# A decoder layer with attention, a selective scan and a quantised feed-forward block: which queues move the rotated heads, and when the feed-forward weights are loaded

## What is computed

```python
x = x + attention(layernorm(x))          # 32 heads of 64, 8 k/v heads, rope on q and k, causal
x = x + ssm(ctx_1024, layernorm(x))      # 16 states: conv, projections, scan over time, gate silu(z)
x = x + ffn(layernorm(x))                # 704 hidden, integer weights of gate, up and down

def step(state, xs):                     # of the ssm, for each of 256 channels and 16 states
    d_t, B_t, C_t, u_t = xs
    dA = jnp.exp(d_t[..., None] * A)
    state = state * dA + (d_t * u_t)[..., None] * B_t[:, None, :]
    y_t = jnp.einsum('ben,bn->be', state, C_t)
    return (state, y_t)

def _qlinear(x, wq, scale):
    W = (wq.astype(jnp.float32) - ZERO_POINT) * scale[:, None]
    return jnp.einsum('bsd,hd->bsh', x, W)
gate = jax.nn.silu(_qlinear(x, wq_gate, s_gate))
up = _qlinear(x, wq_up, s_up)
return _qlinear(gate * up, wq_down, s_down)
```

## Time and profile before

| | before |
|---|---|
| the profiled execution's own time | 523.78 us |
| its span | 522.0 us |
| PE busy | 414.5 us (79%) |
| DVE busy | 366.6 us (70%) |
| ACT busy | 271.0 us (52%) |
| POOL busy | 221.3 us (42%), the issue of DMAs not counted |
| mean granted clock of PE | 0.912 |

### The profile page before, as it was taken

One profiled execution on the slowest core, in us unless ns is written; L12 is line 12 of the kernel. 1 busy time (PEld: TensorE's weight loads), 2 busy tenths in 40 slices (PEclk: granted clock), 3 DMA queues, 4 the chain that ended last, 5 costly groups with the idle time before them and its releaser, 6 DMA issues.

```text
span 522.0 us, 7681 instructions
## 1 busy us (share of the span) xinstructions
PE 414.5 (79%) x2604; PEld 325.4 (62%) x2636; DVE 366.6 (70%) x485; ACT 271.0 (52%) x779; POOL 221.3 (42%) x234
## 2 busy tenths in 40 slices
PE   3648987188768697987889799978998894659996
PEld 1433666166656476866777688757887773447774
DVE  2774357257999885897798679858767999755442
ACT  0514587046556465755666658645556665433321
POOL 1741232206464666446446635635464474310000
PEclk9787789687889799998999989989999997779999
DMA  9325324703151415201430521323042130000000
GB/s 223 74 56 96 113 51 131 230 10 98 37 170 55 156 31 153 96 11 46 133 102 24 144 91 48 76 87 102 21 133 74 57 102 0 2 0 21 20 22 20
DMA packets 51110, 40.63 MB, mean 78 GB/s; under 512 B 32280, under 2 KB 43744, under 8 KB 51072
## 3 DMA queue, kind: packets, MB, share of 16 engines
q1 hardware_dynamic: 40864, 34.48, 23.2%
q0 software_dynamic: 4096, 4.20, 3.4%
q10 hardware_dynamic: 6112, 1.47, 1.4%
HBM read 26.36 MB, written 1.18 MB: 53 GB/s over the span
## 4 chain that ended last, share of the span: by engine, by line
PE 33%; DVE 17%; issue 15%; SPq 12%; POOL 9%; DMA 7%; ACT 5%; ACTq 2%; DVEq 0%; POOLq 0%
PE ps_s L1041 6%; SPq L303 6%; PE ps_p L1028 6%; PE ps_p L1243 5%; DMA qt<-rc 4%; POOL rc L418 4%; DVE state L793 4%; PE ps_s L1228 3%; DVE nmax L711 3%; PE ps_p L1141 3%; PE ps_r L1095 3%; DVE state L786 3%; DMA kt<-rc 3%; SPq L266 2%; POOL y L424 2%
## 5 line engine op out<-in xcount | busy, mean ns | idle before, releaser
L493 ACT ACTIVATE prob<-ps_s,nmax 128x256 f32<-128x256 f32 (+1 forms) x256 | 104.8, 444 | 72.6 <-DVE nmax L711 72.6
L424 POOL TENSOR_TENSOR y<-y,state 128x1024 f32<-128x1024 f32 x32 | 80.3, 2510 | 112.2 <-DVE state L799 112.2
L418 POOL TENSOR_TENSOR rc<-rc,rs 128x512 f32<-128x512 f32 x40 | 57.7, 1442 | 104.0 <-DVE rs L699 70.4
L711 DVE TENSOR_REDUCE nmax<-ps_s 128x2 f32<-128x512 f32 (+1 forms) x96 | 60.3, 682 | 45.1 <-PE ps_s L1052 45.1
L499 ACT ACTIVATE pt<-ps_r 128x512 f32<-128x512 f32 x96 | 53.6, 593 | 58.1 <-PE ps_r L1095 54.5
L793 DVE TENSOR_TENSOR_SCAN state<-decay,state 128x1024 f32<-128x1024 f32 x32 | 81.5, 2546 | 2.3 <-ACT decay L519 1.2
L1041 PE MATMUL ps_s<-kt,qt 64*128 64x256 f32 (+1 forms) x512 | 55.5, 360 | 30.7 <-DMA qt<-rc 30.7
L1028 PE MATMUL ps_p<-xt_all,wq 128*128 128x256 f32 x256 | 71.2, 427 | 9.1 <-DVE rs L703 6.4
L1041 PEld LDWEIGHTS ps_s<-kt,qt 64*128 64x128 f32 x512 | 47.1, 201 | 38.2 <-DMA qt<-rc 32.5
L266 POOL DMA_DIRECT2D qt<-rc x128 | 63.8, 504 | 9.7 <-POOL rc L418 9.5
L1141 PE MATMUL ps_p<-wo,attn_t 128*128 128x256 f32 x256 | 61.7, 389 | 7.7 <-DVE x L816 4.1
(11 more groups left out here) (110 smaller groups left out, 531.1 us busy)
## 6 DMA issues: line engine op xcount, KB each, us to landing
bc<-bc_scratch SPq DMA_DIRECT2D x32, 512.0 KB, 4.7
qt<-rc POOLq DMA_DIRECT2D x128, 32.0 KB, 1.7
qt<-rc SPq DMA_DIRECT2D x128, 32.0 KB, 2.0
kt<-rc SPq DMA_DIRECT2D x64, 32.0 KB, 1.8
kt<-kt SPq DMA_DIRECT2D x8, 256.0 KB, 3.0
wo<-wo_t SPq DMA_DIRECT2D x1, 2048.0 KB, 10.9
wq<-wqkv_t SPq DMA_DIRECT2D x24, 64.0 KB, 2.6
xs<-x SPq DMA_DIRECT2D x1, 1024.0 KB, 8.1
```

The source lines that it names most:

```text
L418: nc.gpsimd.tensor_tensor(rc[:, r % 2, :, :], rc[:, r % 2, :, :], rs[:], ALU.add).then_inc(rope_add, 1)
L424: nc.gpsimd.tensor_tensor(y[:, v % 2, :], y[:, v % 2, :], state[:, v % 2, :], ALU.add).then_inc(state_free, 1)
L493: nc.scalar.activation(o, i, ACT.Exp, bias=nmax[:, r, c:c + 1], accum_out=rsum[:, r, GRP + head:GRP + head + 1]).then_inc(exp_done, 1)
L711: nc.vector.tensor_reduce(nmax[:, u % 2, c:c + k], ps_s[:, part, :].rearrange("p (k s) -> p k s", k=k), AX.X, ALU.max, negate=True).then_i ...
```

## The change

- q: all eight moves of each q are issued by POOL, one after the other; SP issues none. The ropes and scores wait on one semaphore (`q_pool`) in place of two.
- k: the moves are halved. SP issues those of parts 0 and 1, POOL those of parts 2 and 3 (4 DMAs each). The doubling (`double_k`) stays with SP but stands in the next unit of its list.
- SP's list: loads of the feed-forward weights and scales are spread over units 4 to 8; the load of `wo` stands in unit 2; B and C are loaded a unit later in the list; the load of up's weights moves from unit 7 to unit 11. None of these is timed by a unit: SP goes through its list as fast as its waits let it.
- DVE: gate's weights are made floats in unit 10 instead of 5, those of up and down in unit 14 instead of 12.
- ACT: the first activation (L537, which loads the table) stands ahead of the eight weight DMAs of ACT's queue instead of behind them.

```diff
-        def move_heads(queue, u, heads, landed):
+        def move_q(queue, u, heads, landed):
...
+        def move_k(queue, j, heads, landed):
+
+            r = ROPE_AT["k", j]
+            queue.wait_ge(rope_add, r + 1)
+            if j >= 2:
+                queue.wait_ge(score_done, 3 * KG * (j - 1))
+            for i in heads:
+                for c in range(2):
+                    queue.dma_start(kt[c * HALF:(c + 1) * HALF, j % 2, i, :],
+                                    rc[i * HALF:(i + 1) * HALF, r % 2, c, :]).then_inc(landed[j % 2], 16)
...
+            def double_k(j):
+
+                sp.wait_ge(k_sp[j % 2], 16 * k_moves * (j // 2 + 1))
+                sp.wait_ge(k_pool[j % 2], 16 * k_moves * (j // 2 + 1))
                 sp.dma_start(kt[HD:P, j % 2, :, :], kt[0:HD, j % 2, :, :]).then_inc(k_in[j % 2], 16)
...
+            for u in range(UNITS):
+                if u % KG == 2 and u // KG + 1 < GROUPS:
+                    double_k(u // KG + 1)
+                if u < 2:
+                    load_wq(sp, 6 + u)
+                if u == 2:
+                    sp.dma_start(wo[:], wo_t.rearrange("(k p) n -> p k n", p=P)).then_inc(wo_in, 16)
+                load_ffn(u)
+                for v in scans(u - 1) if u else ():
                     if v % 2 == 1 and v // 2 + 2 < NS:
                         sp.wait_ge(hc_done, v + 1)
...
+                        load_bc(v // 2 + 2)
+                if u % KG == 1 and u // KG + 1 < GROUPS:
+                    move_k(sp, u // KG + 1, range(KG // 2), k_sp)
+                if u == 3:
+                    sp.wait_ge(ssm_ready, 5)
+                    load_bc(1)
...
             add_rope(("k", 0))
+            move_k(nc.gpsimd, 0, range(KG // 2, KG), k_pool)
             add_rope(("q", 0))
-            move_heads(nc.gpsimd, 0, range(GRP // 2, GRP), q_in)
+            move_q(nc.gpsimd, 0, range(GRP), q_pool)
...
                 if u + 2 < UNITS:
                     add_rope(("q", u + 2))
-                    move_heads(nc.gpsimd, u + 2, range(GRP // 2, GRP), q_in)
+                    move_q(nc.gpsimd, u + 2, range(GRP), q_pool)
                 if u % KG == 1 and u // KG + 1 < GROUPS:
                     add_rope(("k", u // KG + 1))
+                    move_k(nc.gpsimd, u // KG + 1, range(KG // 2, KG), k_pool)
...
-                if u == 5:
+                if u == 10:
                     dequantise_gate()
-                if u == 12:
+                if u == 14:
                     dequantise_up_down()
```

More of the change, by code:

```diff
@@ L188, in decoder_layer @@
         wv_in = sem("wv_in")
-        q_in = [sem(f"q_in{r}") for r in range(2)]
-        k_half = [sem(f"k_half{r}") for r in range(2)]
+        q_pool = [sem(f"q_pool{r}") for r in range(2)]
+        k_sp = [sem(f"k_sp{r}") for r in range(2)]
+        k_pool = [sem(f"k_pool{r}") for r in range(2)]
         k_in = [sem(f"k_in{r}") for r in range(2)]
@@ L250, in load_wq @@
                                         ).then_inc(wq_in[g], 16)
-        q_moves, k_moves = 2 * GRP, 2 * KG
-        half_moves = q_moves // 2
-        q_low = [sem(f"q_low{r}") for r in range(2)]
-        def move_heads(queue, u, heads, landed):
+        q_moves, k_moves = 2 * GRP, KG
+        def move_q(queue, u, heads, landed):
             r = ROPE_AT["q", u]
@@ new lines, in _, with load_ffn @@
+            full = P * (HT - 1)
+            def load_ffn(u):
+                if u == 4:
+                    sp.dma_start(wgu_i[:], wgate_t.rearrange("(k p) n -> p k n", p=P)).then_inc(ffn_in, 16)
+                elif u == 5:
+                    sp.dma_start(wdn_i[:, 0:HT - 1, :], wdown_t[0:full, :].rearrange("(k p) n -> p k n", p=P)
+                                 ).then_inc(ffn_in, 16)
+                    sp.dma_start(sdn[:], s_down.rearrange("(a n) -> a n", a=1).to_broadcast([P, HID])
+                                 ).then_inc(ffn_in, 16)
+                elif u == 6:
+                    sp.dma_start(wdn_i[0:HP[-1], HT - 1, :], wdown_t[full:HF, :]).then_inc(ffn_in, 16)
+                elif u in (7, 8):
+                    i, v = (0, s_gate) if u == 7 else (1, s_up)
+                    with nc.allow_non_contiguous_dma(reason="704 scales, once"):
+                        sp.dma_start(sgu[:, i, 0:HT - 1], v[0:full].rearrange("(k p) -> p k", p=P)
+                                     ).then_inc(ffn_in, 16)
+                        sp.dma_start(sgu[0:HP[-1], i, HT - 1:HT], v[full:HF].rearrange("(p k) -> p k", k=1)
+                                     ).then_inc(ffn_in, 16)
+                elif u == 11:
+                    sp.wait_ge(wq_done, 1)
+                    sp.dma_start(wgu_i[:], wup_t.rearrange("(k p) n -> p k n", p=P)).then_inc(up_in, 16)
@@ L311, in _ @@
+            move_k(sp, 0, range(KG // 2), k_sp)
+            double_k(0)
             with nc.allow_non_contiguous_dma(reason="weights by the halves of a head, once"):
@@ L343, in _ @@
-            sp.dma_start(sdn[:], s_down.rearrange("(a n) -> a n", a=1).to_broadcast([P, HID])
-                         ).then_inc(ffn_in, 16)
-            move_q(4)
-            move_q(5)
-            sp.wait_ge(ssm_ready, 5)
-            load_bc(1)
-            for u in range(4, UNITS):
-                if u + 2 < UNITS:
-                    move_q(u + 2)
-                if u % KG == 1 and u // KG + 1 < GROUPS:
-                    move_k(u // KG + 1)
-                for v in scans(u):
+            for u in range(UNITS):
[7 more added lines that the diff above has]
+                for v in scans(u - 1) if u else ():
@@ L427, in _ @@
             add_rope(("k", 0))
+            move_k(nc.gpsimd, 0, range(KG // 2, KG), k_pool)
             add_rope(("q", 0))
[L429 removed]
+            move_q(nc.gpsimd, 0, range(GRP), q_pool)
             add_rope(("q", 1))
[L431 removed]
+            move_q(nc.gpsimd, 1, range(GRP), q_pool)
             def x1_rstd(lo, hi, step):
@@ L532, in _ @@
             nc.scalar.dma_start(par[:], ssm_par.rearrange("(e p) n -> p e n", p=P)).then_inc(par_in, 16)
+            act.wait_ge(consts, 2)
+            nc.scalar.activation(rstd2[:], eps[:], ACT.Silu).then_inc(act_warm, 1)
             load_wq(nc.scalar, 2)
             load_wq(nc.scalar, 3)
-            act.wait_ge(consts, 2)
-            nc.scalar.activation(rstd2[:], eps[:], ACT.Silu).then_inc(act_warm, 1)
             act.wait_ge(consts, 6)
```

58 lines of the change are left out of this document (8 added, 50 removed).

## The result

| | before | after |
|---|---|---|
| median of the timed runs | 523.84 us (4 runs) | 496.48 us (4 runs, 496.16 to 497.29) |
| ratio after / before, 95% interval | | 0.946 [0.939, 0.954] |
| the profiled execution's own time, its span | 523.78, 522.0 us | 496.78, 495.0 us |
| mean granted clock of PE | 0.912 | 0.941 |

The change makes the kernel 27.4 us faster, some 5%. The forecast was 494.4 us.

What follows compares the result with a forecast made beforehand. PE was taken to stand 30.7 us for q moves, the stall being made in SP's list. Savings of 2.2 + 0.9 + 11.4 + 11.3 + 2.8 + 0.8 = 29.4 us from 523.8 gave 494.4 us, range 486 to 506.

Steps and rivals of the forecast that it cites:

- A: Start: with ACT's first activation ahead of its weight DMAs, POOL's first sum waits only for the statistics; 2.2 us less.
- B: First scores: k's moves halved and q's eight moves on POOL bring them to 37.2 us; 0.9 us less.
- C: Scores of unit 4: q 4 no longer waits behind the feed-forward loads in SP's list; 11.4 us less.
- D: The five k groups: q stalls shrink to 1.4 us in four, none at unit 28; 11.3 us less with after-effects.
- if moves land in over 2.5 us: Sign against the prediction, for the moves' landing; 1.7 us was assumed, 2.3 us for q 4 beside the load of `wo`.
- E: DVE's floats: up and down in unit 14 save 2.8 us, gate's in a covering v unit 0.8 us.
- POOL as the bound: Rival, all units: POOL's moves stretch; slower by 2% needs 0.91 us per DMA. Chance 0.06 within 2%, 0.02 slower.
- the rule that was set against the change: POOL's moves: each under a two-port operation of VectorE would wait until it ends; the rows showed nothing added.
- the exclusion doesn't bite: Rival, k groups and floats: four stalls are 0.2 us, half the floats' 3.2 us is covered; 488 us, chance 0.14.
- The drive at 2 us or less: Sign for the prediction: DVE's drive in the unit after a k unit takes 2 us or less.
- the loads don't matter: Rival, unit 4: SP would have waited anyway, the gain there is nothing; 506 us, chance 0.06 shared with POOL somewhat slow.
- A new wait in units 0 to 7: Rival: another wait behind q 4 takes back about half of the 11.4 us gained at unit 4; 500 us, chance 0.22.

Runs made afterwards that it cites:

- the ninth move: The changed kernel with one more move of 32 x 128 per q on POOL, into a tile nobody reads: 506.1 us, ratio 0.968.
- q halved again: The changed kernel, but SP issues half of each q's moves again and POOL the other half: 485.7 us, ratio 0.933.

## Why the prediction was right, and where it wasn't

The time (494.4 forecast, 496.5 measured) held, and so did the main mechanism: q was late because of what stood ahead of it in SP's list. Not every step did. Up to unit 8 the gain is 15.6 us, where A, B, C and gate's floats made 15.3 us, and behind it 11.2 us instead of 14.1 us; in C and D it is luck that the size came out. By its steps:

- **A and B, the start: 4.4 us, not 3.1.** POOL's first sum came at 12.06 as said, but k's rope sum started 3.8 us earlier (24.48 instead of 28.24), where A had 2.2 us. A took only the wait from the chain, and the normalisation behind it became 2.75 us shorter; k's rope sum didn't get all of this, since it then stood behind POOL's convolution. B was priced at 0.9 us and is 0.7 us, from that sum to the first scores (11.40 instead of 12.08 us). A was mis-sized. The first scores still wait 5.05 us for q; "no DMA wait" was said.
- **C, unit 4: 11.3 us, forecast 11.4.** The scores start at 89.17 (near 88 was said). They still wait 1.60 us: the last move of q 4 took 5.4 us to land, issued 4.8 us behind the load of `wo` of 2 MB, which itself took 10.2 us; 2.3 us was assumed, and the price of a landing beside a large load was the weak point. The same happened at unit 6 (1.77 us), beside B and C and two of the weight loads. That C's size came out all the same is luck: the after-effect went too, which wasn't in the sum. From scores 4 to scores 5 it was 10.05 us and is 8.59 us. The text had called the prediction wrong "if moves land in over 2.5 us". The median is 1.7 us, but of the last moves for which PE waited, those of units 4, 6, 12, 16 and 24 took 5.4, 5.5, 2.7, 5.7 and 2.9 us.
- **D, the k groups: near in size, by another cause.** The waits ahead of units 12, 20 and 24 are 1.18, 0.68 and 1.31 us against 1.4 us each; at unit 28 there is none, as said, and the scores of all four are 1.58 us long. But the 1.4 us came from an order that didn't happen. D let DVE's drive run between `y` and POOL's rope sum. In all five k groups the drive came last instead: it took 2.80 us, and the rope sum ran at once and at full pace (1.27 us). For that order D has a stall of 0.2 us. The rest is landing: 1.7 us was assumed for the last move, and it took 2.7, 2.3 and 2.9 us. Unit 24, with the drive, the rope sum, the moves and the scores:

```profile
312.09 2.80 DVE L787 TENSOR_TENSOR state<-du,bc 128x1024 f32<-128x1024 f32 x1
312.52 1.27 POOL L417 TENSOR_TENSOR rc<-rc,rs 128x512 f32<-128x512 f32 x1
314.09 3.93 POOL L264 DMA_DIRECT2D qt<-rc  x8 [0.29 <-POOL rc L417]
320.46 1.58 PE L1041 MATMUL ps_s<-kt,qt 64*128 64x256 f32 x16 [1.31 <-DMA qt<-rc]
```

  In these units SP's doubling of k and a load of B and C are issued up to 2.5 us before the first of these moves. With B and C held back the last move of q 20 landed in 1.7 us, but those of q 12 and q 24 still took 2.7 and 2.4 us, so B and C aren't the whole of it; the rest is open. Two terms were missing besides: the two pauses of POOL, with waits of 1.99 and 1.23 us, in plain units that were costed at nothing with a cover of 0.1 us.
- **E, the floats: the step that failed most.** The text let unit 14 cover 1.9 of 5.1 us because DVE has slack over a v unit. From the scores of unit 14 to those of unit 17 it is 36.54 us, against 11.2 + 10.7 + 8.9 = 30.8 us without loss: 5.7 us, where 1.4 + 3.2 = 4.6 were put down. By that alone the step would stand: four kernels that are much the same there lose 3.7 to 5.0 us. With q out of the way the floats alone lose 6.65 us, more than their 5.15 us of work. DVE's slack doesn't help where the delayed instruction is the row maximum, on which the exponentials, their transposes and the values of that very unit hang: PE idles 3.74 us there, and the clock falls behind it: the granted clock of 228 to 235 us was 0.57 in that trace, and a fill of q took 3.53 us instead of 1.99 us. Gate's floats, the smaller part of E, went as said or better: 0.8 us was forecast, and from the scores of unit 5 to those of unit 6, waits left out, it is 12.84 instead of 14.19 us, while units 10 and 11, where they stand now, are no longer than before.
- **From unit 8 to the end** the gain is 11.2 us where D and E said 14.1. The three k groups took 3.2 us instead of 4.2, the pauses 3.2 instead of 0, and units 14 to 17 lost 5.7 instead of 4.6: 3.3 us more, about the 2.9 us that are missing.
- **Waits at PE: 18.9 us, near 10 was said.** 5.05 us are the first scores; the four groups hold 7.3, the landings at units 4 and 6 3.4, the pauses 3.2.

Of the rivals, POOL as the bound was put at 0.91 us per DMA for slower. It didn't come: one move takes 499 ns on average of 256 in the kernel after, with DVE at work beside them, and none took over 0.651 us.

```profile
L264 POOL DMA_DIRECT2D qt<-rc x256: 496/497/651, 29.8 to 394.9; - x128
```

Yet the rule that was set against the change does show, beside one kind of operation. The Trainium skill (SBUF — State Buffer, "SBUF: two separate sides") warns that a DMA from GpSimd's queue starves for descriptors while VectorE runs an operation in a two-port mode. With the ninth move, a q move that began 0.17 us before a TENSOR_SCALAR of DVE took 1.15 us and ended 0.1 us after it:

```profile
187.51 1.15 POOL L266 DMA_DIRECT2D qt<-rc  x1 [1.89 <-issue]
```

```profile
187.68 0.89 DVE L835 TENSOR_SCALAR wgu<-wgu_i 128x1408 f16<-128x1408 int32 x1
```

In the thirteen traces every move of POOL that took over 0.62 us, except the first DMA that POOL issues in each, ran beside a TENSOR_SCALAR, and ended about 0.1 us after it: 1.15 and 1.09 us here, 1.05 us with q halved again, 1.04 us with B and C held back, and the 0.651 us of the kernel after. Beside the other operations of DVE, two-operand ones, scans and maxima, none took over 0.59 us. The traces don't name the mode in which DVE ran them. The change was safe from this rule because hardly a TENSOR_SCALAR runs beside the moves (beside 4 of POOL's 288 in the kernel after), and not because moves never wait for DVE.

The same section's exclusion of two-input operations shows again, but not as the prediction used it (D): the drive, 1.22 us long in most units, is 2.80 us in the k groups, it stood behind two POOL operations in a row, and the scan behind it was not stretched (2.29 us). That is the rival "the exclusion doesn't bite" for POOL's list. Its 488 us didn't come, since the landings took what the order gave, and the floats cost more. "The drive at 2 us or less" failed, and the scan has nothing of the up to 3.5 us.

That the loads don't matter is out: with them and the floats moved the time is 508.6 us, and unit 4 doesn't wait. A new wait in units 0 to 7 came, but small: 1.60 + 1.77 us, both for moves that landed late.

## What to carry to other kernels

Before asking which engine should issue a move, look at what stands ahead of it in its queue: here waits and large loads ahead of q cost more than 20 us (22.0 us went when q alone left that queue), and once they stood behind it, two queues beat one (ratios of 0.933 and 0.946). The slack of an engine over a unit says little about one extra block of work on it; ask which result is late behind the block, and who hangs on it. The same block cost 6.65 us in one unit and under 0.4 us in another. An engine whose list just fits is moved past its edge by 0.8 us in a unit, and by pauses that no list shows.
